# Moving mask steps, square roots, projections and a transpose within the hand-written order of the last two attention blocks

## The chip, the cores and the metric

The kernel runs on one core of a Trainium2 chip. The metric is the device time of one execution in microseconds (us); the lowest, the median and the highest of three runs are given, and the profile is of one execution.

## What is computed

Sixteen sequences of 64 tokens with 256 features pass through six residual layers: cross attention over 1601 context rows, a selective scan layer, a spiking feed-forward layer, windowed cross attention with 16 heads (layer 4), an attention with a phase mask (layer 5) and a mixture of eight experts (layer 6). The change touches the order of layers 4 to 6. Cut to what matters:

```python
# layer 5: attention with a mask from a two-dimensional projection
qp = h @ Wtq.T + btq
diff = qp[:, :, None, :] - qp[:, None, :, :]
dist_sq = sum(diff * diff, -1)
forward_bias = 0.5 * (1.0 + cos(arctan2(diff[..., 1], diff[..., 0])))
threshold = mean(dist_sq) + 1.25 * std(dist_sq)          # over all pairs of one sequence
valid = (dist_sq <= threshold) & causal
weights = softmax(where(valid * forward_bias == 0, -inf, q @ k.T / sqrt(d)))
x = x + weights @ v @ Wo.T + bo + 0.1 * (qp / norm(qp)) @ Wfq.T + bfq    # h is the layer norm of x
# layer 6: every expert is computed, the two best are weighted by their scores
scores = n @ gate_w + gate_b                             # n is the layer norm of x
out = sum over experts e of comb[:, e] * (relu(n @ w1[e] + b1[e]) @ w2[e] + b2[e])
```

## The kernel before

The 1024 tokens lie in 8 tiles of 128, two sequences each. Every engine has a program of its own, written out by hand as a list of calls, and runs it strictly in that order; the engines meet at semaphores only. So a call that is moved in an engine's list changes when everything behind it on that engine may start. Blocks of the program end with a barrier over all engines.

`ffn_and_heads` holds layers 3 and 4 and, at its end, the part of layer 5 for tiles 0 to 3 (the first half) that needs no later tile. For that half, VectorE makes in turn: `phases` (the two projections `qp`), `distances` (`dd`, `dist` and their row sums), `cones` (which pairs lie in the forward half plane, L1989 to L1992, in four operations `ady0`, `ady`, `ok`, `okc`), `spreads` (deviation from the mean and its row sums) and `masks` (variance, threshold, and the mask `k.ok`, L1997 to L2002). Between these stand the last heads' steps: `step(TILES)` and `step(TILES + 1)` with `residual` (L1909) and `divide`, and the layer norm of tiles 4 to 7, which is `deviations(1)` (L1917, L1920), the square root `root(1)` on ScalarE (L1635) and `normalise(1)` (L1925, L1928, four operations `xn`). TensorE turns these four normed tiles with `turn_normed(2)` and `turn_normed(3)` (L1440), two tiles each, both through the one bank `T[1]`, so that ScalarE's copy `move_normed(2)` (L1639) stands between them. The block ends when ScalarE has done `move_normed(3)`.

`phase_and_experts` begins with the attention of the first half (`scores`, `values`, `project_phase`, `weigh`), makes its layer norm with `root(0)` on ScalarE (L2489) and `normalise(0)` on VectorE (L2683 to L2691), and turns it with `turn_normed(0, 0)` and `turn_normed(0, 1)` (L2290). Then the experts of the first half (expert steps 0 to 7) run woven with layer 5 of the second half, and after them steps 8 to 15. An expert step is `hidden(n)` on TensorE (L2328, L2329, L2333: 12 matmuls of 128x512, since each fp32 product is made of three products of rounded parts), `rectify(n)` on ScalarE (L2500, `hid` and `h_hi`), `rest_of_hidden(n)` on VectorE (L2735, `h_lo`), and `output(n)` on TensorE (L2307, 24 matmuls of 128x256), which `add_output(n)` on VectorE adds to `x` (L2758). The rounded parts of a weight come from `large(j)` on ScalarE (L2441, `w_hi`) and, from j = 2 on, a subtraction on GpSimd (L2565, `w_lo`). `project(0)` to `project(3)` are the queries and keys of the second half (L2209), which `move(n)` copies (L2447). `spread_rows` (L2214) needs `diag` from VectorE (L2595). The rounded input `x_lo` of the experts comes from `rest_of_normed` (L2698), after ScalarE's four copies `move_normed` (L2484).

The wait at the head of the turning of normed tiles is this one; tiles 4 and 5 must be normed for `turn_normed(1, 0)`, tiles 6 and 7 for `turn_normed(1, 1)`:

```python
            def turn_normed(h, g):
                e.wait_ge(s_xn, HT * h + 2 * g + 2)
```

Of the kernel before, what the change touches and what calls it, by code (L numbers as in the profile page):

```python
# [14 lines left out]
P = 128  # L15
# [1096 lines left out]
def ffn_and_heads(nc, k):  # L1112
# [7 lines left out]
    with ExitStack() as ctx:  # L1120
# [91 lines left out]
        ac_steps = [("r2", 1), ("x2", 0), ("x2", 1), ("r2", 2), *sq(0), ("x2", 2), ("cv", 0), ("r2", 3), ("y", 0), ("v", 0),  # L1212
                    *sq(1), ("x2", 3), ("r3", 0), ("y", 1), *sq(2), ("x3", 0), ("r3", 1), ("y", 2), *sq(3), ("x3", 1),
                    ("r3", 2), ("y", 3), ("v", 1), ("x3", 2), ("v", 2), ("v", 3), ("r3", 3), ("x3", 3),
                    ("nrm",), ("qk", 0), ("qk", 1), ("qk", 2), ("std",), ("qk", 3)]
        ve_steps = [("rc2", 0), ("xn2", 0), ("ag2", 1), ("ep2", 1), ("rc2", 1), ("xn2", 1), ("rs", 2), ("st2", 2), ("ag2", 2),
                    ("ep2", 2), ("rc2", 2), ("xn2", 2), ("rs", 3), ("st2", 3), ("ag2", 3), ("ep2", 3), ("rc2", 3), ("xn2", 3),
                    ("k", 0), ("cvec", 0), ("st3", 0), *nm(0), ("st3", 1), *nm(1), ("st3", 2), *nm(2), ("k", 1), ("k", 2),
                    ("k", 3), ("st3", 3), *nm(3), ("qp",), ("qsq",), ("nrm2",), ("diag",), ("dd",), ("dq",), ("dist",),
                    ("rowsum",), ("ady0",), ("ady",), ("ok",), ("okc",), ("nrmx",), ("nri",), ("re",), ("mean",), ("dev",),  # L1220
                    ("devsq",), ("rowsq",), ("var",), ("thr",), ("in",), ("ok2",), ("add",)]
        pe_at, ac_at, ve_at = ({step: i + 1 for i, step in enumerate(steps)} for steps in (pe_steps, ac_steps, ve_steps))
        made = {"pe": 0, "ac": 0, "ve": 0}

# [332 lines left out]
        def _(e):  # L1557
# [104 lines left out]
            def move_phase(n):  # L1662
                w, m = n // 2, n % 2
                pe("qk", n)
                done(e.activation((k.w_in[:, m, 0:HALF], k.kT[:, m, :])[w], QK[m], ACT.Identity,
                                  bias=col(k, ("bq5", "bk5")[w], m)), "qk", n)
# [41 lines left out]
            step(TILES + 1)  # L1708
            move_phase(1)
            root(1)  # L1710
            move_phase(2)
            ve("var")
            done(e.activation(std, var, ACT.Sqrt), "std")
            move_phase(3)
            move_normed(2)
            move_normed(3)
# [50 lines left out]
        def _(e):  # L1767
# [7 lines left out]
            def done(ins, *name):  # L1775
                mark(ins, ve_at, "ve", s_fv, *name)
# [136 lines left out]
            def deviations(h):  # L1913
                hs = slice(HT * h, HT * (h + 1))
                e.wait_ge(s_st, HT * (h + 1))
                for t in range(HT * h, HT * (h + 1)):
                    j = e.bn_aggr(mv[:, t, :], k.stats[:, t, :])  # L1917
                j.then_inc(s_ln, 1)
                e.wait_ge(s_ln, 3 * h + 1)
                e.tensor_scalar(veps[:, hs], mv[:, hs, 1], EPS, None, ALU.add).then_inc(s_ln, 1)  # L1920

            def normalise(h):
                hs = slice(HT * h, HT * (h + 1))
                e.wait_ge(s_sd, h + 1)
                e.reciprocal(rstd[:, hs], sd[:, hs]).then_inc(s_ln, 1)  # L1925
                e.wait_ge(s_ln, 3 * h + 3)
                for t in range(HT * h, HT * (h + 1)):
                    e.tensor_scalar(k.xn[:, t, :], k.x[:, t, :], mv[:, t, 0:1], rstd[:, t:t + 1],  # L1928
                                    ALU.subtract, ALU.mult).then_inc(s_xn, 1)
# [18 lines left out]
            def chain(ins, *name):  # L1948
                done(ins, *name)
                own(*name)  # L1950
# [33 lines left out]
                chain(e.tensor_tensor(dev, dev, dev, ALU.mult), "devsq")  # L1984
                done(e.reduce_sum(rowsq, dev, AX.X), "rowsq")

            def cones():
                x, y = by_phase(dd)[:, 0], by_phase(dd)[:, 1]
                chain(e.tensor_scalar(ady, y, -4096.0, None, ALU.mult), "ady0")  # L1989
                chain(e.scalar_tensor_tensor(ady, y, 4096.0, ady, ALU.mult, ALU.max), "ady")  # L1990
                chain(e.scalar_tensor_tensor(k.ok, x, -1.0, ady, ALU.mult, ALU.is_le), "ok")
                done(e.tensor_tensor(k.ok, k.ok, k.causal[:, :].unsqueeze(1).to_broadcast([P, HT, L]), ALU.mult), "okc")  # L1992

            def masks():
                pe("sumsq")
                own("rowsq")
                done(e.tensor_scalar(var, SUMS[:, 128:128 + HT], 1.0 / (n_pairs - 1.0), None, ALU.mult), "var")  # L1997
                ac("std")
                chain(e.scalar_tensor_tensor(limit, std, 1.25, mean, ALU.mult, ALU.add), "thr")
                chain(e.tensor_tensor(dev, dist, wide(limit), ALU.is_le), "in")  # L2000
                chain(e.tensor_tensor(k.ok, k.ok, dev, ALU.mult), "ok2")
                done(e.tensor_scalar(k.ok, k.ok, -NEG, NEG, ALU.mult, ALU.add), "add")  # L2002
# [41 lines left out]
                step(i)  # L2044
            phases()
            distances()
            cones()
            step(TILES)
            spreads()
            step(TILES + 1)  # L2050
            deviations(1)
            normalise(1)
            masks()


def load_matrix(e, k, j):
# [11 lines left out]
def phase_and_experts(nc, k, out):  # L2068
# [5 lines left out]
    with ExitStack() as ctx:  # L2074
# [117 lines left out]
        def _(e):  # L2192
# [11 lines left out]
            def project(n):  # L2204
                w, m = n // 2, n % 2
                if n >= 2:
                    ac("qk", n - 2)
                for c in range(KD):
                    i = e.matmul(BK[QK[n]][:, :], k.w5[w][:, c, m * P:(m + 1) * P], k.xT[:, c, HALF:TOK], start=c == 0, stop=c == 1)  # L2209
                done(i, "qk", n)  # L2210

            def spread_rows():
                ve("diag")
                done(e.matmul(BK[ROW][:, :], k.same_batch[:, :], diag.rearrange("p g t n -> p (g t n)"), start=True, stop=True),  # L2214
                     "row")
# [100 lines left out]
            def hidden(n):  # L2316
                h, x = divmod(n, E)
                if h == 0:
                    split_done(2 * x)
                if x == 0:  # L2320
                    e.wait_ge(s_xh, 4 * h + 2)
                tok = slice(h * HALF, (h + 1) * HALF)
                for m in range(KD):
                    if n:
                        e.wait_ge(s_r, 2 * (n - 1) + m + 1)
                    cols = slice(m * P, (m + 1) * P)
                    for c in range(KD):
                        e.matmul(HB[m][:, :], k.w_hi[x][:, 0, c, cols], k.x_hi[:, c, tok], start=c == 0, stop=False)  # L2328
                        e.matmul(HB[m][:, :], k.w_lo[x][:, 0, c, cols], k.x_hi[:, c, tok], start=False, stop=False)  # L2329
                    if x == 0:  # L2330
                        e.wait_ge(s_xl, 2 * (h + 1))
                    for c in range(KD):
                        i = e.matmul(HB[m][:, :], k.w_hi[x][:, 0, c, cols], k.x_lo[:, c, tok], start=False, stop=c == 1)  # L2333
                    i.then_inc(s_h, 1)
# [24 lines left out]
            def output(n):  # L2359
                h, x = divmod(n, E)  # L2360
                if h == 0:
                    split_done(2 * x + 1)
                e.wait_ge(s_l, 2 * n + 2)
                for g in range(2):
                    e.wait_ge(s_a, 2 * n + g + 1)
                    for u in range(2):
                        tok = slice((2 * g + u) * P, (2 * g + u + 1) * P)
                        for c in range(KD):
                            i = product(OB[g][:, u * D:(u + 1) * D], h_hi[n % 2][:, c, tok], h_lo[n % 2][:, c, tok],
                                        k.w_hi[x][:, 1, c, :], k.w_lo[x][:, 1, c, :], c == 0, c == 1)  # L2370
                    i.then_inc(s_o, 1)
# [13 lines left out]
            turn_normed(0, 0)  # L2385
            turn_normed(0, 1)
            spread_rows()
            hidden(0)
            scores_of_experts(0)
            project(2)  # L2390
            hidden(1)
            project(3)
            values(1, 0)
            values(1, 1)
            batch_sum()
# [17 lines left out]
            hidden(5)  # L2413
            output(4)
            hidden(6)
            output(5)
            turn_normed(1, 0)
            turn_normed(1, 1)
            hidden(7)
            scores_of_experts(1)  # L2420
            output(6)
# [11 lines left out]
        def _(e):  # L2433
# [4 lines left out]
            def large(j):  # L2438

                e.wait_ge(k.s_w[j % SLOTS_W], 16 * (j // SLOTS_W + 1))  # L2440
                e.activation(k.w_hi[j // 2][:, j % 2, :, :], k.raw[j % SLOTS_W][:, :, :], ACT.Copy).then_inc(s_hi, 1)  # L2441
# [45 lines left out]
            def root(h):  # L2487
                e.wait_ge(s_ln, 3 * h + 2)
                e.activation(sd[:, half(h)], veps[:, half(h)], ACT.Sqrt).then_inc(s_sd, 1)  # L2489
# [24 lines left out]
            large(0)  # L2514
            large(1)
            large(2)
            large(3)
            root(0)
            move(0)
            move_normed(0)  # L2520
            move(1)
            norms()
            rectify(0)
            large(4)
            move(2)
            rectify(1)
            move(3)
            move_values(1, 0)
            move_values(1, 1)
            shares_across(0)  # L2530
# [14 lines left out]
            rectify(5)  # L2545
            large(12)
            large(13)
            root(1)
            rectify(6)
            large(14)  # L2550
            move_normed(1)
            large(15)
# [16 lines left out]
        def _(e):  # L2569
# [224 lines left out]
            add_output(3)  # L2794
            rest_of_hidden(5)
            add_output(4)
            normalise(1)
            rest_of_hidden(6)
            add_output(5)
            rest_of_hidden(7)  # L2800
            rest_of_normed(1)
# [268 lines left out]
```

## Time and profile before

| | us |
|---|---|
| lowest, median, highest of three runs | 729.65, 731.73, 735.07 |
| the profiled execution's own time | 729.65 |
| its span (first to last instruction) | 727.9 |
| TensorE busy in the span | 661.8 |
| VectorE busy in the span | 471.3 |
| ScalarE busy in the span | 370.1 |
| GpSimd busy in the span | 223.1 |

The profiled execution is the fastest of the three. 1.75 us of its time lie outside the span. The mean granted TensorE clock was 0.976 of full speed.

### The profile page before, as it was taken

How to read it: one execution, taken by the hardware profiler on the slowest of the kernel's cores; microseconds unless marked ns; L12 is line 12 of the kernel's file. 1: busy time of each engine (PE TensorE's matmuls, PEld its weight loads, DVE VectorE, ACT ScalarE, POOL GpSimd, SP SyncE). 2: the span in 40 equal slices, each digit the busy share in tenths (PEclk: the TensorE clock that was granted, in tenths of full speed). 3: DMA queues.
4: the chain of work that ended last, by engine and by line, in shares of the span. 5: the costliest groups of instructions: out<-in, count | busy, mean ns of one | idle time of the engine just before them, and what ended most of it. 6: DMA issues, size and time to landing. Idle time of an engine off the chain costs nothing. (4 is left out here: it accounts for less than half of the span.)

```text
span 727.9 us, 11207 instructions
## 1 busy us (share of the span) xinstructions
PE 661.8 (91%) x4206; PEld 457.7 (63%) x4206; DVE 471.3 (65%) x803; ACT 370.1 (51%) x675; POOL 223.1 (31%) x181
## 2 busy tenths in 40 slices
PE   3989999999984998898988989899989989999998
PEld 1445555553353556565565778787767666889897
DVE  5123433448637998988989536576787657586554
ACT  1221111215476998888988532432456365357442
POOL 2000000000008999897878000032543002222000
PEclk9999999999996999999999999999999899999999
DMA  8999999738121232222320000000100012110000
GB/s 317 367 373 418 419 420 425 312 104 263 31 86 59 95 109 87 87 100 75 116 87 30 0 1 16 1 0 16 32 3 3 1 59 73 43 59 1 30 1 30
DMA packets 31070, 86.45 MB, mean 119 GB/s; under 512 B 7901, under 2 KB 19577, under 8 KB 28841
## 3 DMA queue, kind: packets, MB, share of 16 engines
q1 hardware_dynamic: 30456, 85.28, 32.2%
q8 instruction: 34, 0.56, 0.3%
q10 hardware_dynamic: 560, 0.46, 0.2%
q14 instruction: 20, 0.16, 0.1%
HBM read 83.50 MB, written 1.11 MB: 116 GB/s over the span
## 5 line engine op out<-in xcount | busy, mean ns | idle before, releaser
L679 POOL TENSOR_TENSOR dbu<-du,bs 128x1024 f32<-128x1024 f32 x64 | 151.0, 2379 | 233.2 <-DVE du L879 214.8
L992 PE MATMUL Y<-weighed,ident 128*128 128x512 f32 (+1 forms) x256 | 101.8, 519 | 0.0
L889 DVE TENSOR_TENSOR_SCAN w_in<-A,dbu 128x1024 f32<-128x1024 f32 x42 | 95.2, 2277 | 0.0
L772 ACT ACTIVATE weighed<-T,CT 128x256 f32<-128x256 f32 x208 | 83.2, 473 | 23.3 <-PE T L982 20.8
L761 ACT ACTIVATE A<-delta,negA 128x504 f32<-128x504 f32 x128 | 83.0, 692 | 3.0 <-DVE xn L889 2.9
L992 PEld LDWEIGHTS Y<-weighed,ident 128*128 128x128 f32 x256 | 44.0, 193 | 29.8 <-issue 29.2
L982 PE MATMUL T<-ident,w_in 128*128 128x128 f32 x336 | 45.8, 281 | 12.3 <-ACT weighed L772 7.3
L982 PEld LDWEIGHTS T<-ident,w_in 128*128 128x128 f32 x336 | 38.0, 144 | 28.5 <-issue 15.7
L889 DVE TENSOR_TENSOR_SCAN xn<-A,dbu 128x1024 f32<-128x1024 f32 x22 | 50.1, 2277 | 2.3 <-POOL dbu L679 2.3
L253 PE MATMUL S<-cT,qkT 128*64 128x512 f32 (+1 forms) x256 | 46.5, 517 | 0.8 <-issue 0.8
L265 PE MATMUL O<-cN,pT 128*64 128x256 f32 x384 | 46.7, 385 | 0.0
L359 ACT ACTIVATE prob<-S,nbias 128x1601 f32<-128x1601 f32 x8 | 12.8, 1597 | 64.7 <-DVE nbias L463 64.7
L2735 DVE TENSOR_TENSOR h_lo<-hid,h_hi 128x512 fp32r<-128x512 f32 x32 | 22.1, 692 | 33.4 <-ACT h_hi L2500 33.4
L456 DVE TENSOR_REDUCE mx<-S 128x1 f32<-128x1601 f32 x8 | 14.6, 1825 | 43.5 <-PE S L253 43.5
L2500 ACT ACTIVATE hid<-BK,cols 128x512 f32<-128x512 f32 x32 | 22.1, 690 | 37.5 <-PE BK L2333 36.2
L982 PE MATMUL T<-ident,xn 128*128 128x128 f32 x176 | 24.2, 282 | 14.9 <-DVE xn L889 9.3
L2307 PE MATMUL BK<-w_hi,h_hi 128*128 128x256 f32 x128 | 37.6, 294 | 0.1
L2307 PE MATMUL BK<-w_lo,h_hi 128*128 128x256 f32 x128 | 36.9, 289 | 0.0
L2307 PE MATMUL BK<-w_hi,h_lo 128*128 128x256 f32 x128 | 36.9, 288 | 0.0
L253 PEld LDWEIGHTS S<-cT,qkT 128*64 128x64 f32 x256 | 17.2, 139 | 30.4 <-issue 30.2
L2565 POOL TENSOR_TENSOR w_lo<-raw_w,w_hi 128x512 fp32r<-128x512 f32 x14 | 17.7, 1278 | 60.2 <-ACT w_hi L2441 60.2
L1742 POOL TENSOR_TENSOR w_in<-qkb,trig 128x512 f32<-128x512 f32 x8 | 10.5, 1319 | 79.5 <-DVE qkb L1869 79.5
(393 smaller groups left out, 1350.8 us busy)
## 6 DMA issues: line engine op xcount, KB each, us to landing
cT<-in_ctxT SPq DMA_DIRECT2D x8, 3202.0 KB, 14.6
cN<-in_ctx SPq DMA_DIRECT2D x8, 3072.0 KB, 13.8
bs<-b_rows SPq DMA_DIRECT2D x32, 512.0 KB, 3.6
raw_w<-in_w SPq DMA_DIRECT2D x16, 256.0 KB, 2.8
w<-in_w SPq DMA_DIRECT2D x7, 256.0 KB, 8.3
vs<-vx SPq DMA_DIRECT2D x8, 136.0 KB, 2.3
x<-in_x SPq DMA_DIRECT2D x2, 512.0 KB, 6.1
cR<-in_ctx SPq DMA_DIRECT2D x1, 1024.0 KB, 32.2
```

The lines of the kernel that those rows point to most:

```text
L253: j = e.matmul(S[64 * b:64 * b + 64, c * HALF:c * HALF + w], qkT[:, kt, q:q + 64], cT[r][:, b, kt, c * HALF:c * HALF + w], start=kt == 0, ...
L265: j = e.matmul(O[64 * b:64 * b + 64, 0:D], pT[0:n_keys(c), c, 64 * b:64 * b + 64], v, start=c == 0, stop=c == ROWS)
L679: e.tensor_tensor(dbu[s % NB][:, :, :], half(m.du, s // DS), row, ALU.mult).then_inc(s_bu, 1)
L761: i = e.activation(by_batch(A[s % 2][:, j * HALF:(j + 1) * HALF]), by_batch(m.delta[:, c, h * HALF:(h + 1) * HALF]), ACT.Exp, scale=m.negA ...
L772: i = e.activation(weighed[s % 2][:, q * Q:(q + 1) * Q], T[:, q * Q:(q + 1) * Q], ACT.Copy, scale=c_of(s, q))
L889: e.tensor_tensor_scan(S[s % NS], A[s % 2][:, :], dbu[s % NB][:, :, :].rearrange("p c n -> p (c n)"), 0.0, ALU.mult, ALU.add).then_inc(s_h, 1)
L982: i = e.transpose(T[:, q * Q + j * P:q * Q + (j + 1) * P], S[s % NS][:, j * HALF + q * P:j * HALF + (q + 1) * P], k.ident[:, :])
L992: e.matmul(Y[:, w], k.ident[:, :], weighed[s % 2][:, w], start=False, stop=True, skip_group_check=True).then_inc(s_y, 1)
L2307: ins = e.matmul(dst, a, b, start=first and i == 0, stop=last and i == 2)
L2500: i = e.activation(dst, HB[m][:, :], ACT.Relu, bias=col(k, "b1", 2 * x + m))
L2565: e.tensor_tensor(k.w_lo[j // 2][:, j % 2, :, :], k.raw[j % SLOTS_W][:, :, :], k.w_hi[j // 2][:, j % 2, :, :].bitcast(F32), ALU.subtract). ...
L2735: e.tensor_tensor(h_lo[n % 2][:, m, :], hid[m][:, :], h_hi[n % 2][:, m, :].bitcast(F32), ALU.subtract).then_inc(s_l, 1)
```

## The change

Only the order of calls changes, in both functions; every operation is still made, and none is added. In `ffn_and_heads` the four `cones` operations of VectorE go behind `deviations(1)` and join `masks`, and the whole of `masks` now stands before `normalise(1)`; ScalarE takes the root `std` before `move_phase(2)`. In `phase_and_experts` TensorE does `project(2)` before `hidden(0)`, `project(3)` before `hidden(1)`, and the two `turn_normed(1, ...)` before `output(5)`; ScalarE does `move(0)` before `root(0)`, `large(3)` behind both, `move(1)` before `move_normed(0)`, and `root(1)` behind `rectify(6)`; VectorE does `normalise(1)` behind `rest_of_hidden(6)`.

```diff
@@ ffn_and_heads: ScalarE
             root(1)
-            move_phase(2)
             ve("var")
             done(e.activation(std, var, ACT.Sqrt), "std")
+            move_phase(2)
             move_phase(3)
@@ ffn_and_heads: VectorE
-            def cones():
+            def masks():
                 x, y = by_phase(dd)[:, 0], by_phase(dd)[:, 1]
                 chain(e.tensor_scalar(ady, y, -4096.0, None, ALU.mult), "ady0")
                 chain(e.scalar_tensor_tensor(ady, y, 4096.0, ady, ALU.mult, ALU.max), "ady")
-                chain(e.scalar_tensor_tensor(k.ok, x, -1.0, ady, ALU.mult, ALU.is_le), "ok")
-                done(e.tensor_tensor(k.ok, k.ok, k.causal[:, :].unsqueeze(1).to_broadcast([P, HT, L]), ALU.mult), "okc")
-
-            def masks():
                 pe("sumsq")
                 own("rowsq")
                 done(e.tensor_scalar(var, SUMS[:, 128:128 + HT], 1.0 / (n_pairs - 1.0), None, ALU.mult), "var")
+                chain(e.scalar_tensor_tensor(k.ok, x, -1.0, ady, ALU.mult, ALU.is_le), "ok")
+                chain(e.tensor_tensor(k.ok, k.ok, k.causal[:, :].unsqueeze(1).to_broadcast([P, HT, L]), ALU.mult), "okc")
                 ac("std")
...
             distances()
-            cones()
             step(TILES)
             spreads()
             step(TILES + 1)
             deviations(1)
+            masks()
             normalise(1)
-            masks()
@@ phase_and_experts: TensorE
             spread_rows()
+            project(2)
             hidden(0)
             scores_of_experts(0)
-            project(2)
+            project(3)
             hidden(1)
-            project(3)
...
             hidden(6)
-            output(5)
             turn_normed(1, 0)
             turn_normed(1, 1)
+            output(5)
             hidden(7)
@@ phase_and_experts: ScalarE
             large(2)
+            move(0)
+            root(0)
             large(3)
-            root(0)
-            move(0)
+            move(1)
             move_normed(0)
-            move(1)
             norms()
+            move(2)
             rectify(0)
             large(4)
-            move(2)
+            move(3)
             rectify(1)
-            move(3)
...
+            rectify(6)
             root(1)
-            rectify(6)
             large(14)
@@ phase_and_experts: VectorE
             add_output(4)
+            rest_of_hidden(6)
             normalise(1)
-            rest_of_hidden(6)
             add_output(5)
```

The first place is VectorE at the end of `ffn_and_heads`. `hmv` and `hveps` are the mean, variance and variance plus epsilon of tiles 4 to 7, `w_xp` holds the mask `k.ok`, and the lines L1989 to L1992 of before stand 18 rows further up. Before:

```order
L1909 TENSOR_TENSOR x<-x,hX 128x256
L81 BN_STATS stats<-x 128x6
L1917 BN_AGGR hmv<-stats 128x2 x4
L1920 TENSOR_SCALAR hveps<-hmv 128x4
L1925 RECIPROCAL hrstd<-hsd 128x4
L1928 TENSOR_SCALAR xn<-x,hmv,hrstd 128x256 x4
L1997 TENSOR_SCALAR small<-hS 128x4
L1999 SCALAR_TENSOR_TENSOR small<-small 128x4
L2000 TENSOR_TENSOR xz<-rows,small 128x256
L2001 TENSOR_TENSOR w_xp<-w_xp,xz 128x256
L2002 TENSOR_SCALAR w_xp<-w_xp 128x256
```

The same place after the change:

```order
L1920 TENSOR_SCALAR hveps<-hmv 128x4
L1989 TENSOR_SCALAR xz<-xz 128x256
L1990 SCALAR_TENSOR_TENSOR xz<-xz 128x256
L1993 TENSOR_SCALAR small<-hS 128x4
L1994 SCALAR_TENSOR_TENSOR w_xp<-xz 128x256
L1995 TENSOR_TENSOR w_xp<-w_xp,causal 128x256
L1997 SCALAR_TENSOR_TENSOR small<-small 128x4
L1998 TENSOR_TENSOR xz<-rows,small 128x256
L1999 TENSOR_TENSOR w_xp<-w_xp,xz 128x256
L2000 TENSOR_SCALAR w_xp<-w_xp 128x256
L1925 RECIPROCAL hrstd<-hsd 128x4
L1928 TENSOR_SCALAR xn<-x,hmv,hrstd 128x256 x4
```

Nine operations have come between the variance and the four `xn`.

The second place is ScalarE near the start of `phase_and_experts`: the roots, copies and weight roundings around `root(0)`, which writes `sd`. Before:

```order
L2441 ACTIVATE w_hi<-raw_w 128x512 x4
L2489 ACTIVATE sd<-veps 128x4
L2447 ACTIVATE w_in<-BK,cols 128x512
L2484 ACTIVATE x_hi<-BK 128x2x256 x2
L2484 ACTIVATE xT<-BK 128x2x256 x2
L2447 ACTIVATE w_in<-BK,cols 128x512
L2456 ACTIVATE nrm<-nrm 128x4
```

The same place after the change:

```order
L2438 ACTIVATE w_hi<-raw_w 128x512 x3
L2444 ACTIVATE w_in<-BK,cols 128x512
L2486 ACTIVATE sd<-veps 128x4
L2438 ACTIVATE w_hi<-raw_w 128x512
L2444 ACTIVATE w_in<-BK,cols 128x512
L2481 ACTIVATE x_hi<-BK 128x2x256 x2
L2481 ACTIVATE xT<-BK 128x2x256 x2
L2453 ACTIVATE nrm<-nrm 128x4
```

The root now stands behind the first copy of a projection, and the fourth weight rounding behind the root.

The third place is VectorE around the layer norm of the second half, `normalise(1)` of `phase_and_experts` (`mv`, `veps`, `rstd`, `xn`). Before:

```order
L2735 TENSOR_TENSOR h_lo<-hid,h_hi 128x512 x2
L2758 SCALAR_TENSOR_TENSOR x<-BK,comb,x 128x256 x4
L2683 BN_AGGR mv<-stats 128x2 x4
L2686 TENSOR_SCALAR veps<-mv 128x4
L2688 RECIPROCAL rstd<-sd 128x4
L2691 TENSOR_SCALAR xn<-x,mv,rstd 128x256 x4
L2735 TENSOR_TENSOR h_lo<-hid,h_hi 128x512 x2
L2758 SCALAR_TENSOR_TENSOR x<-BK,comb,x 128x256 x4
```

The same place after the change:

```order
L2732 TENSOR_TENSOR h_lo<-hid,h_hi 128x512 x2
L2755 SCALAR_TENSOR_TENSOR x<-BK,comb,x 128x256 x4
L2732 TENSOR_TENSOR h_lo<-hid,h_hi 128x512 x2
L2680 BN_AGGR mv<-stats 128x2 x4
L2683 TENSOR_SCALAR veps<-mv 128x4
L2685 RECIPROCAL rstd<-sd 128x4
L2688 TENSOR_SCALAR xn<-x,mv,rstd 128x256 x4
L2755 SCALAR_TENSOR_TENSOR x<-BK,comb,x 128x256 x4
```

The four `xn`, for which `turn_normed(1, ...)` waits on TensorE, stand behind the second pair of `h_lo`, that of `hidden(6)`; on TensorE `turn_normed(1, ...)` has moved the other way, up past the 24 matmuls of `output(5)`.

## Rows read from the trace of the kernel before

**Rows 1.** The page, its first part: busy time of each engine

```profile
PE 661.8 (91%) x4206; PEld 457.7 (63%) x4206; DVE 471.3 (65%) x803; ACT 370.1 (51%) x675; POOL 223.1 (31%) x181
```

**Rows 2.** Chain that ended last, 662 to 667 us: start, duration, what

```profile
662.54 2.88 PE BK L2307 x24
665.41 0.87 PE BK L2290 x8
666.28 0.23 PE BK L2328
```

**Rows 3.** Timeline of TensorE, end of `ffn_and_heads`: start, duration, line, [idle before <- releaser]

```profile
577.22 2.07 PE L1428 MATMUL hX<-w,honT 128*128 128x256 f32 x4
...
587.89 0.60 PE L1440 MATMUL hT<-ident,xn 128*128 128x128 f32 x4
589.41 0.63 PE L1440 MATMUL hT<-ident,xn 128*128 128x128 f32 x4 [0.92 <-ACT xT L1639]
590.98 1.15 PE L2233 MATMUL BK<-w_out,w_in 128*64 128x64 f32 x32 [0.94 <-PEq L1120]
```

**Rows 4.** Timeline of VectorE, the same stretch

```profile
577.77 0.28 DVE L1989 TENSOR_SCALAR xz<-xz 128x256 f32<-128x256 f32 x1
...
579.35 0.41 DVE L1909 TENSOR_TENSOR x<-x,hX 128x256 f32<-128x256 f32 x1
...
586.42 1.39 DVE L1928 TENSOR_SCALAR xn<-x,hmv,hrstd 128x256 f32<-128x256 f32 x4
...
588.15 0.16 DVE L1999 SCALAR_TENSOR_TENSOR small<-small 128x4 f32<-128x4 f32 x1 [0.27 <-ACT small L1713]
...
589.26 0.29 DVE L2002 TENSOR_SCALAR w_xp<-w_xp 128x256 f32<-128x256 f32 x1
```

**Rows 5.** Timeline of ScalarE around `root(0)` of `phase_and_experts`

```profile
603.73 0.20 ACT L2489 ACTIVATE sd<-veps 128x4 f32<-128x4 f32 x1 [2.67 <-DVE veps L2686]
604.21 0.69 ACT L2447 ACTIVATE w_in<-BK,cols 128x512 f32<-128x512 f32 x1 [0.28 <-PE BK L2209]
```

**Rows 6.** Timeline of VectorE, the operation that `spread_rows` needs

```profile
605.95 0.75 DVE L2595 TENSOR_TENSOR cn<-qp,diag 128x256 f32<-128x256 f32 x2
```

**Rows 7.** Timeline of TensorE, `spread_rows` to `scores_of_experts(0)`

```profile
606.76 1.12 PE L2214 MATMUL BK<-cn,same_batch 128*128 128x512 f32 x2
...
609.32 0.73 PE L2333 MATMUL BK<-x_lo,w_hi 128*128 128x512 f32 x2 [0.52 <-DVE x_lo L2698]
...
611.27 1.84 PE L2301 MATMUL BK<-wg,xT 128*128 128x8 f32 x16
```

**Rows 8.** Timeline of ScalarE around `root(1)` of `phase_and_experts`

```profile
658.60 1.28 ACT L2489 ACT_TABLE_LOAD   x1
...
663.16 0.68 ACT L2500 ACTIVATE h_hi<-BK,cols 128x512 fp32r<-128x512 f32 x1
```

**Rows 9.** Timeline of VectorE around `normalise(1)` of `phase_and_experts`

```profile
659.94 0.37 DVE L2683 BATCH_NORM_AGGREGATE mv<-stats 128x2 f32<-128x6 f32 x4
...
661.18 1.38 DVE L2691 TENSOR_SCALAR xn<-x,mv,rstd 128x256 f32<-128x256 f32 x4
...
663.88 0.69 DVE L2735 TENSOR_TENSOR h_lo<-hid,h_hi 128x512 fp32r<-128x512 f32 x1 [0.69 <-ACT h_hi L2500]
```

**Rows 10.** Timeline of all engines: one `xn` of layer 4 beside a GpSimd operation

```profile
532.60 1.26 POOL L1742 TENSOR_TENSOR w_in<-qkb,trig 128x512 f32<-128x512 f32 x1 [4.34 <-DVE qkb L1869]
...
532.89 1.12 DVE L1854 TENSOR_SCALAR xn<-x,mv,rstd 128x256 f32<-128x256 f32 x1
```

**Rows 11.** Timeline of GpSimd, the `w_lo` that follows `large(14)`

```profile
664.44 1.29 POOL L2565 TENSOR_TENSOR w_lo<-raw_w,w_hi 128x512 fp32r<-128x512 f32 x1 [3.77 <-ACT w_hi L2441]
```

**Rows 12.** Windows: PE, PEld, DVE, ACT, POOL busy, granted clock, DMA share, GB/s

```profile
532.40:535.80 3.40, 3.40 (x16) 2.35 (x14) 3.16 (x6) 3.07 (x5) 3.14 (x4) 0.53 0.00 0
573.40:580.30 6.90, 6.90 (x40) 4.30 (x41) 4.59 (x12) 1.48 (x2) 0.00 (x0) 0.52 0.00 0
```

**Rows 13.** Timeline of TensorE, the longest wait of layer 4

```profile
529.85 0.66 PE L1354 MATMUL hT<-ident,hrot 128*128 128x128 f32 x4 [2.80 <-DVE hrot L1878]
```

More of the change, by code:

```diff
@@ L1214, in ffn_and_heads @@
                     ("r3", 2), ("y", 3), ("v", 1), ("x3", 2), ("v", 2), ("v", 3), ("r3", 3), ("x3", 3),
-                    ("nrm",), ("qk", 0), ("qk", 1), ("qk", 2), ("std",), ("qk", 3)]
+                    ("nrm",), ("qk", 0), ("qk", 1), ("std",), ("qk", 2), ("qk", 3)]
         ve_steps = [("rc2", 0), ("xn2", 0), ("ag2", 1), ("ep2", 1), ("rc2", 1), ("xn2", 1), ("rs", 2), ("st2", 2), ("ag2", 2),
@@ L1219, in ffn_and_heads @@
                     ("k", 3), ("st3", 3), *nm(3), ("qp",), ("qsq",), ("nrm2",), ("diag",), ("dd",), ("dq",), ("dist",),
-                    ("rowsum",), ("ady0",), ("ady",), ("ok",), ("okc",), ("nrmx",), ("nri",), ("re",), ("mean",), ("dev",),
-                    ("devsq",), ("rowsq",), ("var",), ("thr",), ("in",), ("ok2",), ("add",)]
+                    ("rowsum",), ("nrmx",), ("nri",), ("re",), ("mean",), ("dev",), ("devsq",), ("rowsq",), ("ady0",), ("ady",),
+                    ("var",), ("ok",), ("okc",), ("thr",), ("in",), ("ok2",), ("add",)]
         pe_at, ac_at, ve_at = ({step: i + 1 for i, step in enumerate(steps)} for steps in (pe_steps, ac_steps, ve_steps))
```

## The prediction

> **What bounds the kernel now.** I read the page first: TensorE is busy 91% of the span [rows 1]. Then the chain that ended last: around the second transpose of normed tiles it goes from one TensorE row to the next with no gap [rows 2]. Then the timelines of TensorE, VectorE and ScalarE over the two places where calls move. They show that nearly every moved call lies where TensorE, the engine that sets the end, waits for nothing or for little: 0.92 and 0.94 us at the end of `ffn_and_heads` [rows 3] and 0.52 us in `hidden(0)` [rows 7]. The change adds and removes no work, so it can win only from these short waits, and it loses wherever a moved call now makes TensorE stand. The question at each place is: who releases TensorE, and by how much is that releaser early or late?
>
> **End of `ffn_and_heads`.** The four `cones` operations took from 577.77 to 579.35, 1.58 us [rows 4]. Taking them away there brings nothing: the `residual` behind them needs `project_out(6)`, which TensorE ended at 577.22 + 2.07 = 579.29 [rows 3]. Behind `deviations(1)` they do cost, together with the rest of `masks`: from the threshold at 588.15 to the end of `add` at 589.26 + 0.29 are 1.40 us [rows 4]. The wait for `std` (0.27) lies under `ok` and `okc`, which now stand between `var` and the threshold; `var` itself is under 0.1 us behind its neighbour. So 1.58 + 1.40 = 3.0 us come in front of `normalise(1)`. The four `xn` begin at 589.4 instead of 586.42. They take 1.39 us for four [rows 4], so about 0.32 from one to the next and 0.42 each, and the second is done 0.74 us after the first has begun: `turn_normed(2)` can start at 590.15. Before it started at 587.89, and from there to the first matmul of the next block passed 3.09 us [rows 3], of which 0.2 us was ScalarE's copy held up by a projection's copy that will now be long gone. So the next block starts at 590.15 + 2.9 = 593.05 instead of 590.98: **+2.1 us**. The `std` that is done earlier on ScalarE is waited for by nobody on the path. Bounds: had TensorE run at full clock from 573.4 to 580.3 (it had 0.52 [rows 12]), `project_out(6)` would have been done over a microsecond earlier, and the `cones` would have been in the way of the chain residual, transpose, output projection; up to 1.3 us of the loss would come back. Lower bound 0.8, upper 2.3.
>
> **Front of `phase_and_experts`.** `root(0)` ran at 603.73, in time for the variance. Now it stands behind `move(0)`, which waited for TensorE and started at 604.21 [rows 5]; with some 0.59 us until the next can start, the root comes at 604.8, 1.07 us later. All of VectorE behind it moves too, and `diag`, ready at 605.95 + 0.75 = 606.70 [rows 6], was just in time for `spread_rows` at 606.76 [rows 7]. So TensorE is 1.07 us late there.
>
> A second loss hangs on `large(3)`, which now follows the root and so brings its GpSimd half to 605.6 to 606.9, upon the four `xn` at 605.25 to 606.6. In layer 4, one `xn` that began while GpSimd was at work took 1.12 us and ended just behind it [rows 10], where one takes about 0.42 with GpSimd still (this is the 1.39 for four [rows 4]). I take the last two `xn` as held to the end of the GpSimd operation: 606.9 + 0.73 = 607.6 instead of 606.6, **+1.0** more. The Trainium skill says the same of the port ("GPSIMD Engine Reference", section 1, Specifications): the SBUF interface of GpSimd is shared with VectorE, with contention for VectorE operations in a two-port mode or with two SBUF inputs. By that rule both ends of the collision count; without it this term would be 0 and the same term below too.
>
> The gain is `project(2)` in front of `hidden(0)`: it fills the time in which `x_lo` is made. From 606.76 to 611.27 are 4.51 us [rows 7]; the work in them is 12 matmuls at 0.23 [rows 2], 2.8 us, and about 0.8 of `spread_rows` (listed as 1.12, its tail overlapped). So 0.9 us of waiting go. The four copies and both `x_lo` are then ready by about 609.6 (610.6 with the collision), and `hidden(0)` starts not before 610.4. `project(3)` waits for `move(1)` only, long done; `rectify(0)`, for which `hidden(1)` waits, is covered by the gate scores and `project(3)`. Sum of the front: 1.07 + 1.0 - 0.9 = **+1.2 us**; bounds 0.2 and 2.
>
> **The second half's layer norm.** This is the largest term. `hidden(6)` ended at 662.54, and `output(5)` filled TensorE until 665.41, when the eight transposes came and found their input ready (0.87 us, no wait) [rows 2]: VectorE had begun the four `xn` at 661.18 [rows 9]. Both ends move against each other. TensorE now wants them at 662.54. VectorE now does `rest_of_hidden(6)` first, whose second operation waits for `h_hi`, made by ScalarE at 663.16 + 0.68 [rows 8], and starts at 663.88 [rows 9]. With 0.6 until the next starts, `normalise(1)` begins at 664.5. From its first operation to the first `xn` passed 661.18 - 659.94 = 1.24 us [rows 9], part of it again stretched by GpSimd; I take 1.1, so the `xn` begin at 665.6. The square root's table load (1.28 us [rows 8]) follows `rectify(6)` and ends at about 665.0, when `veps` is ready: it hides. Tile 5 is normed at 665.6 + 0.74 = 666.3, where TensorE has stood for 3.8 us; tile 7 at 667.0, and the transposes end at 667.4. Without a wait they would have ended at 662.54 + 0.87 = 663.4. **+4.0 us**. Queued behind the waiting transpose on TensorE is `output(5)`, which was ready, and everything after it; nothing else can fill the gap.
>
> Here too a GpSimd operation comes over the `xn`: `large(14)` stands behind `root(1)`, so its `w_lo` (1.29 us [rows 11]) no longer starts at 664.44 but at 666.0, between the second and the third `xn`. If it holds them up, tile 7 is ready at 667.3 + 0.73 = 668.05, **+1.1** more. I take it. Bounds of this place: 4.0 and 5.1. Later steps have slack: the gate scores, `x_lo` and the choice of experts all move by the same amount as TensorE.
>
> **The clock.** In 532.4 to 535.8 the granted clock was 0.53, half of 2.4 GHz, in 573.4 to 580.3 it was 0.52 [rows 12]. The first followed the longest wait of layer 4, 2.80 us up to 529.85 [rows 13]; waits of 0.92 and 0.94 were followed by no fall [rows 3]. The change makes a wait of 3.8 us and, at the block's end, one of about 2.3 with two short ones close behind. A spell like the first costs 3.4 x 0.5 = 1.7 us where TensorE is the bound. I take **one spell more, +1.7**; bounds none and three. The Trainium skill ("TensorE: Matmul & The Clock Gate", Part 1) says that the throttled state is the default and that activity releases it. By that rule both new waits would bring a spell, and the sum would be 1.7 us higher; without it, 1.7 lower.
>
> **The sum.** 2.1 + 1.2 + 4.0 + 1.1 + 1.7 = 10.1 us on the profiled execution's own 729.65, so 739.7. That execution is the lowest of three; the median lies 2.1 us above it, and nothing in the change removes what makes it so. I forecast the median: 731.73 + 10.1 = 741.8, rounded to **741.5**.
>
> **Rivals.** *Stalls only:* neither the collisions with GpSimd nor a new clock spell. 731.73 + 2.1 + 0.2 + 4.0 = 738.0, and 736.7 where the `cones` give their 1.3 back. For it speaks that GpSimd might find the port taken and wait itself, and that a spell was seen after 2.8 us of waiting only once. *More cold spells:* both waits and the thin work behind the barrier bring spells, three in all: 741.8 + 3.4 = 745.2. By the clock page's rule this has its weight; against it, part of a spell at the block's start lies beside VectorE and ScalarE work. *Faster:* the spell of 6.9 us at 573.4 depends on thin work before it; if with the changed order TensorE stayed at full clock there, 3.4 us return, and with them 1.3 of the `cones` term; and if ScalarE and VectorE ran so far ahead that the second norm were ready at 662.54, its 5.1 would go. These are 9.8 us against the 8.4 of stalls; it decides only where more than 8.4 of them come true: 731.73 + 8.4 - 9.8 = 730.3. Against it: nothing before 577.77 is touched, and VectorE cannot run ahead of `h_hi`.
>
> **How the numbers follow.** Forecast (all stalls, one or two spells, 739.5 to 744): 0.55. Stalls only (736 to 739.5): 0.30. More spells (744 to 746.5): 0.10. Faster or level (about 730): 0.05. About 1%, 7.3 us, is what a measurement of this kernel can tell from no change: above 739.05 lie the forecast, the third case and a little of the second, 0.62; below 724.4 next to nothing, 0.03. The range is 736 to 745, which leaves out the last case and half of the one before.
>
> **What would show it.** In the profile after: `turn_normed(1, 0)` (L2287) with some 3.8 us idle before it, released by `xn`; the first matmul of `phase_and_experts` about 2.1 us later than 590.98; `x_lo` gone from TensorE's waits and `cn` (`diag`) in its place with about a microsecond or two; `xn` of either norm longer than 1.4 us for four where GpSimd works. The prediction is wrong if `turn_normed(1, ...)` waits less than 3 us, or if the moved spells of the clock weigh more than all stalls.

## The result, and the profile after

| | before | after |
|---|---|---|
| median of the runs | 731.73 us | 743.88 us (five runs, 740.92 to 746.35) |
| ratio, 95% interval | | 1.0168 (1.0137 to 1.0200) |
| span of the profiled execution | 727.9 us | 741.1 us |
| mean granted TensorE clock | 0.976 | 0.968 |

The changed kernel is slower by 12 us, 1.7%. The forecast was 741.5 with a range of 736 to 745. One cause carries most of it: the layer norm of the second half came late where TensorE had nothing else to do. One of the ten executions of `only_turn_moved`, further down, took 2311 us and is left out of its ratio. First TensorE's timeline of the changed kernel, in the order of the places (start, duration, line, idle before and its releaser):

```profile
578.39 2.07 PE L1428 MATMUL hX<-w,honT 128*128 128x256 f32 x4
...
591.05 0.66 PE L1440 MATMUL hT<-ident,xn 128*128 128x128 f32 x4 [1.88 <-DVE xn L1928]
592.49 0.63 PE L1440 MATMUL hT<-ident,xn 128*128 128x128 f32 x4 [0.78 <-ACT xT L1639]
594.06 1.15 PE L2230 MATMUL BK<-w_out,w_in 128*64 128x64 f32 x32 [0.94 <-PEq L1120]
...
610.14 1.30 PE L2287 MATMUL BK<-ident,xn 128*128 128x128 f32 x8 [1.17 <-DVE xn L2688]
611.93 1.12 PE L2211 MATMUL BK<-cn,same_batch 128*128 128x512 f32 x2 [0.49 <-DVE cn L2592]
...
671.79 1.97 PE L2287 MATMUL BK<-ident,xn 128*128 128x128 f32 x8 [4.89 <-DVE xn L2688]
```

Beside [rows 3] and [rows 7], four waits for VectorE have come (1.88, 1.17, 0.49 and 4.89 us), and the one for `x_lo` (0.52) is gone. Next the chain that ended last, around the second norm, where [rows 2] had 2.88, 0.87 and 0.23 us one behind the other:

```profile
666.46 0.47 PE BK L2330 x2
666.92 0.02 issue
666.95 0.69 ACT hid L2497
667.63 0.58 ACT h_hi L2497
668.21 0.02 issue
668.23 1.28 ACT L2486
669.51 0.01 issue
669.52 0.21 ACT sd L2486
669.74 0.02 issue
669.76 0.19 DVE rstd L2685
669.95 0.03 issue
669.98 0.04 DVE xn L2688
670.01 0.29 issue
670.30 1.45 DVE xn L2688
671.75 0.04 issue
671.79 1.97 PE BK L2287 x8
673.76 4.18 PE BK L2304 x24
677.94 0.23 PE BK L2325
```

The chain has left TensorE for 4.9 us: from the last matmul of `hidden(6)` over ScalarE's `hid`, `h_hi`, table load and root to VectorE's `xn`, and back. The table load stands on this chain with its 1.28 us, but it hid nearly all of them, as forecast: VectorE had `veps`, for which the root waits too, at 669.26 + 0.17 = 669.43, and the load ended at 669.51. Behind the wait even the 24 matmuls of `output(5)` took 4.18 us in place of 2.88. VectorE's and GpSimd's timelines show why the `xn` of both norms were long:

```profile
608.33 2.41 DVE L2688 TENSOR_SCALAR xn<-x,mv,rstd 128x256 f32<-128x256 f32 x4
...
669.26 0.17 DVE L2683 TENSOR_SCALAR veps<-mv 128x4 f32<-128x4 f32 x1
...
669.98 2.41 DVE L2688 TENSOR_SCALAR xn<-x,mv,rstd 128x256 f32<-128x256 f32 x4
```

```profile
608.67 1.27 POOL L2562 TENSOR_TENSOR w_lo<-raw_w,w_hi 128x512 fp32r<-128x512 f32 x1 [3.70 <-ACT w_hi L2438]
...
670.33 1.26 POOL L2562 TENSOR_TENSOR w_lo<-raw_w,w_hi 128x512 fp32r<-128x512 f32 x1 [5.24 <-ACT w_hi L2438]
```

Four `xn` took 2.41 us where they took 1.38 [rows 9], and in both cases a `w_lo` had started some 0.34 us behind the first of them. In the chain above the second `xn` is the long one: 1.45 us, with its end at 671.75, 0.16 us behind the end of the `w_lo`. The windows of the granted clock (PE, PEld, DVE, ACT, POOL busy, clock, DMA share, GB/s):

```profile
532.40:535.80 3.40, 3.40 (x44) 2.96 (x41) 2.79 (x4) 3.23 (x5) 3.31 (x4) 0.50 0.00 0
574.00:577.00 3.00, 2.47 (x12) 0.97 (x12) 0.83 (x4) 2.04 (x3) 0.00 (x0) 0.54 0.00 0
669.90:676.70 6.80, 4.91 (x23) 4.91 (x24) 2.79 (x6) 3.04 (x6) 2.00 (x2) 0.51 0.00 0
693.90:697.30 3.40, 3.40 (x10) 2.65 (x9) 0.12 (x1) 1.27 (x2) 0.00 (x0) 0.53 0.04 14
```

The first two lie in the spells (stretches at half clock, 1.2 GHz) of [rows 12], which are there in both kernels, but the first one was longer this time. The same window of layer 4, in the kernel before and then in the changed one:

```profile
531.00:532.00 1.00, 1.00 (x52) 0.96 (x48) 1.00 (x1) 0.98 (x2) 0.00 (x0) 1.00 0.07 16
```

```profile
531.00:532.00 1.00, 1.00 (x24) 1.00 (x22) 1.00 (x2) 0.98 (x2) 0.00 (x0) 0.50 0.00 0
```

In windows of 0.5 us the clock before was at half from 532.2 to 535.6, and in the changed kernel from 529.9 to 536.7. The last two rows are new: TensorE ran at half clock from 669.8, within the wait, to 676.6, 1.3 us before the end of `output(5)`, and once more 17 us later, where in the trace of before it did not.

**Where the 13.2 us between the spans went.** The last output projection of layer 4 but one started at 577.22 before [rows 3] and at 578.39 now: +1.2 us ahead of everything that was changed. From there to the next block's first matmul 15.67 us instead of 13.76: +1.9. From there to the end of `hidden(6)` 72.86 instead of 71.56: +1.3. From there to `hidden(7)` 11.02 instead of 3.74 [rows 2]: +7.3. From there to the end of the span 63.16 instead of 61.62: +1.5. The three in the middle, 10.5 us, are the places of the change. The first and the last are work that it does not touch, and both have the size of a spell: the one in layer 4 was 3.4 us longer in this execution, which is worth at most 1.7 us, and the one at 693.9 (3.4 us at half clock) was not there before. Neither needs the change. Up to that output projection all fourteen traces run the same order, and it started anywhere from 575.3 to 579.6. And a spell at the place of the one at 693.9, behind the eight matmuls of L2352 (L2355 before), stands in five other traces, also where the second norm is as before, as in `front_gpsimd_clear`:

```profile
685.00:686.00 1.00, 1.00 (x4) 0.81 (x3) 0.00 (x0) 0.39 (x1) 0.00 (x0) 0.50 0.00 0
```

### The profile page after: what moved, and what is told of

It reads as the page before. It is cut to its first block and busy times, and to the rows that moved or that the text cites. A ratio compares the mean times of both kernels' runs of the same rounds, so it can differ in the third digit from the quotient of the medians.

```text
span 741.1 us, 11208 instructions
## 1 busy us (share of the span) xinstructions
PE 667.4 (90%) x4206; PEld 461.4 (62%) x4206; DVE 475.0 (64%) x803; ACT 370.7 (50%) x675; POOL 223.2 (30%) x181
```

## Experiments

All times are medians, and ratios are to the kernel before, with 95% intervals. The kernel before had a median of 731.1 in the group of runs of the three parts and `without_second_norm`, 729.8 in that of the second norm taken apart and 731.4 in the last one. A cost with a plus sign is what the ratio makes of that median; it is not the difference of the two medians, and where executions fall into clusters it can be well off it (`only_norm_moved`: +3.1 us by the ratio, 5.0 us between the medians).

### The three parts, each alone

`end_of_heads_only` has the change in `ffn_and_heads` only (its hunks in the diff above).

> Only the part at the end of ffn_and_heads is changed. Theory (nine mask operations stand in front of the four xn): TensorE waits about 1.9 us for xn before turn_normed(2), the first matmul of the next block comes 2 us later than in the kernel before, the total 0 to 4 us more (2 us plus or minus a clock spell). Rival (the total is made by clock spells alone): no wait for xn, no shift. Everything after the barrier should stand as before.

Measured: 733.85 us, 1.0043 (1.0028 to 1.0058), +3.1 us. TensorE's timeline has the same wait as after the whole change, 1.88 us before `turn_normed(2)`:

```profile
588.40 0.66 PE L1440 MATMUL hT<-ident,xn 128*128 128x128 f32 x4 [1.88 <-DVE xn L1928]
589.84 1.08 PE L1440 MATMUL hT<-ident,xn 128*128 128x128 f32 x4 [0.78 <-ACT xT L1639]
591.87 1.97 PE L2230 MATMUL BK<-w_out,w_in 128*64 128x64 f32 x32 [0.94 <-PEq L1120]
```

In this execution the clock fell behind the wait, in the window 589.1 to 595.9:

```profile
589.10:595.90 6.80, 5.12 (x44) 4.13 (x45) 1.96 (x4) 3.73 (x7) 0.98 (x2) 0.50 0.41 105
```

The 32 small matmuls of `scores(0)` took 1.97 us there instead of 1.15. So this part costs its 2 us, and in this execution there was a spell on top. That the spell belongs to the part is not shown: in the traces of `second_norm_only`, `second_norm_filler` and `no_late_norms`, where this place is as before, the clock also fell here, for 3.4 us, behind the old waits of 0.92 and 0.94. The row of `second_norm_only`:

```profile
594.00:595.00 1.00, 1.00 (x15) 0.72 (x13) 0.28 (x1) 0.37 (x2) 0.00 (x0) 0.50 0.93 257
```

The rival (clock alone) falls: the wait is there.

`front_only` has the hunks of `phase_and_experts` from `spread_rows()` to `move(3)` only.

> Only TensorE's project(2) and project(3) and ScalarE's order around root(0) are changed. Theory: spread_rows starts 2.1 us later from the block's start than before, the four xn of the first half take 2.4 us in place of 1.38 because large(3)'s subtraction on GpSimd falls on them, the wait for x_lo is gone, and values(1, 0) starts 1.2 to 1.3 us later from the block's start. Rival (the project moves win more than the root loses): values(1, 0) starts no later than before.

Measured: 732.03 us, 1.0027 (1.0006 to 1.0048), +2.0 us (the medians are 0.9 us apart). `values(1, 0)` starts 620.78 - 591.21 = 29.57 us from the block's start where it started 28.28 us from it: +1.3, as expected. The rival falls.

```profile
607.29 1.30 PE L2290 MATMUL BK<-ident,xn 128*128 128x128 f32 x8 [1.17 <-DVE xn L2691]
609.08 1.12 PE L2214 MATMUL BK<-cn,same_batch 128*128 128x512 f32 x2 [0.49 <-DVE cn L2595]
...
620.78 3.61 PE L2253 MATMUL BK<-w5v,xT 128*128 128x256 f32 x16
```

`second_norm_only` has the hunks around `turn_normed(1, ...)`, `root(1)` and `normalise(1)` only.

> Only turn_normed(1, ...), root(1) and normalise(1) of phase_and_experts are changed. Theory: the wait for xn behind hidden(6) is 3.8 to 5 us, hidden(7) starts about 6 us later than before counted from hidden(6)'s end, 7.3 us if the clock falls to half in the wait, and the total is 6 to 9 us more. This part alone makes over half of the change's cost. Rival (the parts only cost together): under 3 us.

Measured: 740.53 us, 1.0132 (1.0104 to 1.0159), +9.7 us. The wait for `xn` is 4.9 us, the transposes take 1.97 and `output(5)` 4.04 us. From the end of `hidden(6)` to `hidden(7)` are 676.65 - 665.78 = 10.87 us instead of 3.74, +7.1, as expected; the total lies above the expected 6 to 9. This part alone makes about four fifths of the change's cost. What the three ratios add to 1 comes to 0.020 together, and the whole change has 0.017.

`without_second_norm` is the changed kernel with that part put back.

> The changed kernel with the order around the second norm put back. Theory (the costs add up): 3 to 4 us over the kernel before, 7 to 9 us under the changed one; no wait for xn behind hidden(6). Rival: the cost of the second norm comes from what is late ahead of it, and stays.

Measured: 734.21 us, 1.0045 (1.0014 to 1.0076), +3.3 us. The wait behind `hidden(6)` is gone, and the kernel is 9.7 us under the changed one, a little more than the 7 to 9 expected. The costs add up within the intervals; the rival falls.

### The second norm taken apart

`only_turn_moved` moves the transposes alone:

```diff
             hidden(6)
-            output(5)
             turn_normed(1, 0)
             turn_normed(1, 1)
+            output(5)
             hidden(7)
```

> Only TensorE's two turn_normed(1, ...) stand before output(5); ScalarE and VectorE are as in the kernel before. Theory (the loss comes from moving both ends against each other): the second pair of xn is ready at about the end of hidden(6), so the wait is under 0.5 us and the total within 1 us of the kernel before. Rival (taking output(5) out from before the transposes costs by itself): 2 us or more.

Measured: 730.84 us, 1.0005 (0.9977 to 1.0033). The chain that ended last has no wait:

```profile
663.17 0.87 PE BK L2290 x8
664.04 2.88 PE BK L2307 x24
```

`only_norm_moved` moves the other end alone:

```diff
+            rectify(6)
             root(1)
-            rectify(6)
...
+            rest_of_hidden(6)
             normalise(1)
-            rest_of_hidden(6)
```

> Only root(1) and normalise(1) stand later, TensorE is as in the kernel before, with output(5) ahead of the transposes. Theory: the same late xn, but output(5) covers 2.9 us of the wait, so 1 us of waiting stays if GpSimd is out of the way and 2 us if large(14)'s subtraction falls on the xn; the total 1 to 2.5 us more than before, and no clock spell. Rival (the late norm costs as much wherever TensorE waits): 5 us or more.

Measured: 734.83 us, 1.0043 (1.0009 to 1.0076), with `output(5)` ahead of a wait of 2.0 us:

```profile
669.30 1.30 PE L2290 MATMUL BK<-ident,xn 128*128 128x128 f32 x8 [2.02 <-DVE xn L2691]
```

The four `xn` took 2.41 us here too. Two points of the expectation were wrong: the clock did fall, from 670.4 to 673.8, and the total lies above the 1 to 2.5 us, though its interval reaches into them. Moving TensorE's end costs nothing that the runs show, moving the other end costs 3.1 us (0.7 to 5.6), moving both 9.7.

`second_norm_gpsimd_clear` is `second_norm_only` with one call more moved:

```diff
             large(13)
+            large(14)
             rectify(6)
             root(1)
-            large(14)
```

> As second_norm_only, but large(14) stands before rectify(6), so that its subtraction on GpSimd is done before the four xn. Theory of the shared port: the four xn take 1.38 us in place of 2.41, the wait is shorter by 1.0 us and the total by about 1 us. Rival (the xn are long for another reason, as the late table load): 2.4 us as before.

Measured: 737.86 us, 1.0089 (1.0055 to 1.0123). The rows of VectorE, TensorE and GpSimd:

```profile
667.35 1.38 DVE L2691 TENSOR_SCALAR xn<-x,mv,rstd 128x256 f32<-128x256 f32 x4
```

```profile
668.13 1.97 PE L2290 MATMUL BK<-ident,xn 128*128 128x128 f32 x8 [3.86 <-DVE xn L2691]
```

```profile
659.90 3.78 POOL L2565 TENSOR_TENSOR w_lo<-raw_w,w_hi 128x512 fp32r<-128x512 f32 x3 [6.05 <-ACT w_hi L2441]
```

The `xn` take 1.38 us as soon as no `w_lo` runs beside them, and TensorE's wait is 3.9 us instead of 4.9. The table load was as late as before and is not the reason. That the ratio fell by 0.43% (3 us) is more than this 1.0 us, but the two intervals leave room for it.

`second_norm_filler` is `second_norm_only` with twelve matmuls whose results nothing reads, in two banks that the transposes then overwrite:

```diff
+            def filler():
+                ve("x", 1, 1)
+                for g in range(2):
+                    for c in range(6):
+                        e.matmul(BK[XN[1][g]][:, :], k.w_hi[6][:, 0, c % 2, 0:P], k.x_hi[:, c % 2, 0:HALF], start=c == 0,
+                                 stop=c == 5)
...
             hidden(6)
+            filler()
             turn_normed(1, 0)
```

> As second_norm_only, but twelve matmuls of 128x512, whose results nothing reads and which are then overwritten, stand between hidden(6) and turn_normed(1, 0); they take 2.8 us of the wait. Theory (the wait pulls the granted clock to half, which costs 1.3 us in output(5) and some in the transposes): the granted clock stays at full, output(5) takes 2.9 us instead of 4.2, and the total is 1 to 2.5 us less than that of second_norm_only. Rival (the spell of the clock there is chance and not from the wait): no difference in the mean, or more.

Measured: 736.43 us, 1.0075 (1.0045 to 1.0105). The kernel does more work and its median is 4.1 us under that of `second_norm_only`. The two stand in different groups of runs; measured against the kernel before in its own group, the distance is 9.4 us there and 6.6 here. The chain and TensorE's timeline:

```profile
671.82 1.30 PE BK L2290 x8
673.11 2.88 PE BK L2307 x24
```

```profile
666.77 2.88 PE L2377 MATMUL BK<-x_hi,w_hi 128*128 128x512 f32 x12
671.82 1.30 PE L2290 MATMUL BK<-ident,xn 128*128 128x128 f32 x8 [2.17 <-DVE xn L2699]
```

Filler and wait together are about as long as the wait alone was, but `output(5)` is back at 2.88 us and the transposes at 1.30 instead of 1.97. So the spell is there in the three traces in which TensorE stood for 3.9 to 4.9 us, and is not there in the one in which TensorE had work first. A wait of 2.17 us is left in it, and `only_norm_moved` had a spell behind 2.02, so chance is not excluded by one trace. These rows show (1.97 - 1.30) + (4.04 - 2.88) = 1.83 us, less the 2.88 + 2.17 - 4.9 = 0.15 us that filler and wait are longer than the wait alone was, so 1.7 us. The ratios are further apart, but their intervals just meet at 1.0104 and 1.0105.

### The other two places taken apart

`front_gpsimd_clear` is `front_only` with `large(3)` put back before `move(0)`.

> As front_only, but large(3) stands before move(0) again, so that its subtraction on GpSimd is over before the four xn of the first half. Theory of the shared port: the four xn take 1.38 us again, spread_rows comes 1.0 us earlier than in front_only, and the front is level with the kernel before (0.1 to 0.3 us later counted from the block's start to values(1, 0)). Rival: xn stay at 2.4 us.

Measured: 731.79 us, 1.0012 (0.9982 to 1.0042). `xn` take 1.38 us, `spread_rows` starts 609.09 - 592.25 = 16.84 us from the block's start instead of 17.87, and `values(1, 0)` 28.53 us from it, 0.25 later than before the change. The root's 1.07 us and the collision's 1.03 are thus apart, and `project(2)` earns the first back but for 0.25 us.

`project_first_only` has one call moved:

```diff
             spread_rows()
+            project(2)
             hidden(0)
             scores_of_experts(0)
-            project(2)
             hidden(1)
```

> The kernel before with only TensorE's project(2) in front of hidden(0); ScalarE keeps root(0) first. Theory: the wait for x_lo goes, nothing else is late, values(1, 0) starts 0.9 us earlier counted from the block's start, the total is 0.5 to 1 us less, which the runs can hardly tell from nothing. Rival (the gain of the move was bought only with the late root): no shift.

Measured: 729.57 us, 0.9969 (0.9940 to 0.9998). `values(1, 0)` starts 619.67 - 592.18 = 27.49 us from the block's start, 0.8 earlier than before. It is the one part of the change that wins, and its 0.8 us are hardly told from nothing by the runs.

`cones_late_only` moves the four `cones` operations behind `normalise(1)`, with `masks` behind them.

> Only cones moves, behind normalise(1), with masks behind it as before. Theory (the early place of cones was free, and the loss at this place comes from standing in front of xn): no wait for xn before turn_normed(2), the block ends 0 to 0.3 us later because the masks now end after ScalarE's last copy, the total is level. Rival (cones in its early place held up the residual): the residual starts earlier and the total falls by up to 1.5 us.

Measured: 731.75 us, 1.0004 (0.9977 to 1.0032). There is no wait for `xn`, but the block does end later: 591.41 - 586.38 = 5.03 us from `turn_normed(2)` instead of 3.09. I had overlooked a wait of ScalarE, for which TensorE then waits:

```profile
587.97 0.20 ACT L1713 ACTIVATE small<-small 128x4 f32<-128x4 f32 x1 [2.42 <-DVE small L1997]
588.08 0.67 ACT L1665 ACTIVATE w_out<-hS,cols 128x512 f32<-128x512 f32 x1
588.65 0.59 ACT L1639 ACTIVATE xT<-hT 128x512 f32<-128x512 f32 x1
```

```profile
589.38 1.09 PE L1440 MATMUL hT<-ident,xn 128*128 128x128 f32 x4 [2.41 <-ACT xT L1639]
```

The root `std` waits for `var`, which now stands behind `cones`, and `move_phase(3)` and `move_normed(2)` queue behind it. So the early place of `cones` is free only for VectorE, and TensorE's wait is 2.41 us instead of 0.92, +1.5. The rest of the 1.9 us is the clock, which fell in this trace too: the second transposes took 1.09 us instead of 0.63. Whether this shows in the total the interval cannot tell. The `residual` starts no earlier: its wait for the projection (1.47 us) fills the place of `cones`. The rival falls.

`no_late_norms` keeps every TensorE move in `phase_and_experts` and ScalarE's earlier copies, and leaves all norms and the end of `ffn_and_heads` as before:

```diff
             large(3)
             root(0)
             move(0)
+            move(1)
             move_normed(0)
-            move(1)
             norms()
+            move(2)
             rectify(0)
             large(4)
-            move(2)
+            move(3)
             rectify(1)
-            move(3)
```

> All TensorE moves of the change in phase_and_experts and ScalarE's earlier copies, but root(0) before move(0), root(1) and normalise(1) where they stood, and the end of ffn_and_heads as before. Theory (all cost of the change comes from norms made late, none from TensorE's order): no wait for xn anywhere, no wait for x_lo, 0.5 to 1 us under the kernel before and 12 us under the changed one. Rival: TensorE's order costs by itself, 2 us or more over the kernel before.

Measured: 730.86 us, 0.9980 (0.9950 to 1.0011), no wait for `xn` or `x_lo`. So TensorE's new order costs nothing that the runs show as long as the norms come as early as before; the loss needs VectorE's and ScalarE's later norms. How much it then is depends on TensorE's order, as `only_norm_moved` (+3.1) and `second_norm_only` (+9.7) show. The kernel is not told from `project_first_only` or from the kernel before.

## Why the prediction was right

Direction, size and mechanism held. The three places together cost 10.5 us in the profile, where the forecast had 10.1.

- **End of `ffn_and_heads`**, forecast +2.1: +1.9 between the two anchors in the profile, with a wait of 1.88 us for `xn`; by the runs of this part alone +3.1 (2.0 to 4.2). The `xn` came 2.7 us later and not 3.0: counted from the output projection they began at 590.26 - 578.39 = 11.87 us instead of 586.42 - 577.22 = 9.20 ([rows 3] and [rows 4]). The 0.27 us that VectorE had waited for the root before it normed had gone as well.
- **Front**, forecast +1.2 as 1.07 + 1.0 - 0.9: +1.3. The experiments part it into 1.07, 1.03 and -0.8.
- **Second norm without the clock**, forecast 4.0 + 1.1: the wait of 4.89 us plus 0.43 for the second pair (1.30 - 0.87 in the run with the filler, at full clock) are 5.3. One detail was off: I let the collision hit the last two `xn`, with 3.8 us for the first wait. The `w_lo` started 0.35 us behind the first `xn` and hit the second, as the forecast's own 0.4 us should have told me with 0.32 us from one `xn` to the next. So nearly all of it lay in the first wait; `second_norm_gpsimd_clear` has the 3.9.
- **The clock**, forecast one spell, +1.7: behind the long wait it cost 2.0 us (transposes 1.97 instead of 1.30, `output(5)` 4.18 instead of 2.88). Here the size came out near by luck: the forecast took a spell of 3.4 us, and this one lasted 6.8, of which 2.0 lay in the wait, where they cost nothing. That it belongs to the wait is borne out by the filler, in one trace. The forecast also built on waits of 0.92 and 0.94 us that no fall followed; in three other traces one did. And behind the wait of 2.80 us in layer 4 the clock stayed up in the trace of `only_turn_moved`: the length of the wait alone does not settle whether a spell follows.
- **What is missing from the forecast** is the difference of 743.88 to 741.8, 2.1 us. In the profiled execution 2.7 us came from spells in work that was not moved, the longer one in layer 4 and the one at 693.9; both also stand in traces of kernels without the second norm's move, so they are not shown to be the change's. How much of the 2.1 us such spells make in the median stays open. The rival *more cold spells* (745.2) had the number of spells right and the places wrong: in this trace none came at the barrier. The one for *stalls only* is excluded by the clock rows; of *faster* nothing was seen: the spell from 574 is still there.
- **The chances** were added up wrongly: the forecast (0.55) and *more spells* (0.10) both lie above 739.05 whole, so at least 0.65 stood there and not 0.62.

The Trainium skill says that the throttled state is the default and that activity releases it ("TensorE: Matmul & The Clock Gate", Part 1). The prediction took this to mean a spell behind both new waits, which the Trainium skill does not say there. The trace of the changed kernel has one behind the 4.89 us, and none behind the 1.88 us at the barrier; that of `end_of_heads_only` has one there, too. The Trainium skill also has the SBUF interface of GpSimd shared with VectorE, with contention for VectorE operations in a two-port mode or with two SBUF inputs ("GPSIMD Engine Reference", section 1, Specifications). The traces agree that GpSimd's operation holds up VectorE's: 2.41 against 1.38 us. Which of the two conditions the `xn` meet no run here shows.

## What to carry to other kernels

Where one engine is the bound, look for the few operations on other engines that it waits for, and put nothing in front of them: here the same norm was free, cost 3 us or cost 10 us, depending only on what the two ends had in front of them. Be wary of moving both ends of a transfer between engines toward each other. TensorE's end alone was free, since the norm was ready early, and the norm's end alone cost a third, since independent work (`output(5)`) covered 2.9 us of the wait. A wait can cost more than its length: behind 4.9 us of standing, half clock cost 2.0 us more. And a GpSimd operation of 1.26 us that slid over four short VectorE operations made them 1.03 us longer. Count such costs between two fixed places within a trace: spells elsewhere move whole executions of one and the same kernel by more (728.1 to 734.7 us in 31 runs of the kernel before).

## What was unexpected

Twelve useless matmuls went with a ratio 0.6% lower (1.0132 to 1.0075, with intervals that just meet), and a wait of only 2.0 us was followed by half clock in `only_norm_moved`. Four `xn` beside a GpSimd subtraction took 2.40 to 2.41 us in six kernels, and 1.38 without it: 1.03 us more, beside a subtraction of 1.26.
